# Cross-attention and FFN stack: first-batch clears, weight fetch, key mask, residual adds and squares moved

## What is computed

```python
# L0x (8 heads of 16) and L1x (16 heads of 8): attention of 256 queries on 512 keys
q, k, v = x @ Wq.T + bq, ctx @ Wk.T + bk, ctx @ Wv.T + bv
scores = einsum('bqhd,bkhd->bhqk', q, k) / scale
scores = scores + ((1.0 - attention_mask) * -10000.0)[:, None, None, :]   # L1x only
out = einsum('bhqk,bkhd->bqhd', softmax(scores), v)
# L0f, two layers of local attention and a gated unit
q, k, v = split(shift_token(x) @ wqkv, 3)
q, k = rotary(q / norm(q) * qs, k / norm(k) * ks)     # norm over each head's 64 columns
x = x + local_attention(q, k, v) @ wo                  # window of 64
x = x + (a * gelu(g)) @ w2 + b2                        # a, g from layernorm(shift_token(x))
# L3f: causal attention, 16 heads of 8, and a mixture of experts; both with a residual
```

## Time and profile before

| what | value |
|---|---|
| median of 3 runs | 3030.18 us (3027.31 to 3030.22) |
| the profiled execution | 3025.31 us |
| its span | 3023.5 us |
| mean granted clock of TensorE | 0.893 of full speed |
| PE busy | 2394.9 us, 79% |
| DVE busy | 1631.5 us, 54% |
| ACT busy | 1275.0 us, 42% |
| POOL busy | 941.1 us, 31% |

### The profile page before, as it was taken

How to read it: one execution, slowest core, us unless ns; L and a number is a source line. 1 busy time by engine, 2 the same in 40 slices (tenths; PEclk the granted TensorE clock), 3 DMA queues, 4 the chain that set the end, 5 groups by cost and what they waited for, 6 DMA issues and landing times. The chain is left out here.

```text
span 3023.5 us, 46226 instructions
## 1 busy us (share of the span) xinstructions
PE 2394.9 (79%) x16127; PEld 1479.8 (49%) x16128; DVE 1631.5 (54%) x3753; ACT 1275.0 (42%) x2869; POOL 941.1 (31%) x913
## 2 busy tenths in 40 slices
PE   2973677667655998799749879879999998389698
PEld 1431455345532443566537656546666665245465
DVE  4767764566444775433465444445555554566433
ACT  1652565256522665222214322246666665125222
POOL 1414772377202331000000000037676776044000
PEclk7986898789976999899879889979999999589899
DMA  5610000000012330000010000010000000042000
GB/s 135 81 19 6 1 1 1 0 1 1 1 60 39 45 43 10 15 0 0 0 47 1 1 29 0 0 61 1 1 1 1 1 1 1 5 49 35 1 0 14
DMA packets 49811, 53.80 MB, mean 18 GB/s; under 512 B 9264, under 2 KB 47920, under 8 KB 48720
## 3 DMA queue, kind: packets, MB, share of 16 engines
q1 hardware_dynamic: 42992, 41.68, 8.4%
q0 software_dynamic: 4896, 8.81, 0.9%
q10 hardware_dynamic: 1728, 0.79, 0.2%
HBM read 24.25 MB, written 1.05 MB: 8 GB/s over the span
## 5 line engine op out<-in xcount | busy, mean ns | idle before, releaser
L1946 POOL TENSOR_SCALAR L3x_prob<-L3x_prob,L3x_inverse 128x512 f32<-128x512 f32 x256 | 395.8, 1565 | 184.1 <-DVE L3x_inverse L2124 184.1
L1065 DVE TENSOR_TENSOR W_probT<-W_prob,W_pS 128x512 f32<-128x512 f32 (+1 forms) x232 | 159.4, 687 | 367.9 <-ACT W_prob L1050 367.9
L1050 ACT ACTIVATE W_prob<-W_pS 128x512 f32<-128x512 f32 (+1 forms) x232 | 138.5, 597 | 455.9 <-PE W_pS L1021 455.9
L1031 PEld LDWEIGHTS W_pT<-fw,W_probT 128*128 128x128 f32 (+1 forms) x1856 | 241.9, 191 | 115.9 <-issue 107.4
L1020 PE MATMUL W_pS<-hT,fw 128*128 (+1 forms) x464 | 241.2, 602 | 26.0 <-DVEq L484 26.0
L1031 PE MATMUL W_pT<-fw,W_probT 128*128 128x128 f32 (+1 forms) x1856 | 246.2, 276 | 6.2 <-DVE W_probT L1065 6.2
L2086 DVE CUSTOM_DVE_ANT_0 L3x_prob<-L3x_pS,L3x_mask_now 128x512 f32<-128x512 f32 x256 | 166.0, 686 | 147.5 <-PE L3x_pS L1954 147.5
L1021 PE MATMUL W_pS<-hT,fw 128*128 (+1 forms) x464 | 239.3, 598 | 0.0
L2031 ACT ACTIVATE L3x_prob<-L3x_prob,L3x_row_top 128x512 f32<-128x512 f32 x256 | 183.2, 716 | 73.0 <-DVE L3x_row_top L2086 73.0
L855 DVE TENSOR_REDUCE L1x_row_top<-L1x_pS 128x2 f32<-128x1024 f32 x128 | 156.6, 1223 | 74.3 <-PE L1x_pS L671 73.9
L800 ACT ACTIVATE L1x_prob_by_key<-L1x_pX 128x512 f32<-128x512 f32 x256 | 148.5, 596 | 101.8 <-PE L1x_pX L678 100.5
(11 more groups left out here) (363 smaller groups left out, 5188.6 us busy)
## 6 DMA issues: line engine op xcount, KB each, us to landing
L0x_key_stack<-xw SPq DMA_DIRECT2D x48, 128.0 KB
L1x_key_stack<-xw SPq DMA_DIRECT2D x96, 64.0 KB
L3f_stacks<-L3f_qk_part SPq DMA_DIRECT2D x96, 64.0 KB
fw<-in_f_L3f SPq DMA_DIRECT2D x1, 4483.5 KB, 13.4
fw<-in_f_L1f POOLq DMA_DIRECT2D x1, 4359.0 KB, 13.7
fw<-in_f_L0f POOLq DMA_DIRECT2D x1, 3890.0 KB, 12.4
fw<-in_f_L2f SPq DMA_DIRECT2D x1, 3460.0 KB, 10.8
L0x_query_stack<-xw SPq DMA_DIRECT2D x42, 64.0 KB
```

The source lines that it names most:

```text
L1031: last = pe.matmul(m.pT[:, e % 2, t * C:(t + 1) * C], hidden[0:size, s, t * P:(t + 1) * P], down(i), start=i == 0 and t == 0, stop=i == PI ...
L1050: act.activation(gated[0:size, s, 0:GROUP], prod[0:size, s, :], func, bias=bias).then_inc(activated, 1)
L1065: ins = dve.tensor_tensor(hidden[0:size, s, 0:GROUP], gated[0:size, s, 0:GROUP], prod[0:size, 2 + s, :], ALU.mult)
L1946: pool.tensor_scalar(prob(u, h, t), prob(u, h, t), m.inverse[:, u % 2, h, t:t + 1], None, ALU.mult).then_inc(a.normed, 1)
```

## The change

Five edits. In the narrow attentions DVE clears only the first key buffer ahead of the first query copy, POOL the first query buffer; the other clears follow the copy of batch 0. SP's wait for the clears counts to 2b + 1 in place of 2(b + 1), and ACT's waits for POOL's. The weight fetch goes from POOL's first place to behind the last split step of batch 1. L1x's mask is made and stored in the norm phase, and its phase goes. In the local attentions the squares of the first two batches are made by ACT from PSUM (activation Square, next to the copy), later ones by POOL as before. The two add phases go: the sum is DVE's first operation in the second gated unit of L0f and in L3f's experts, whose output now goes to x. In L3f's attention two of three stack clears, `pO` and the value tile follow batch 0's last add.

```diff
-def prepare(nc, m, name):
+def prepare(nc, m, name, mask=None):
...
+            @ph.block.sync
+            def _(sp):
+                sp.dma_start(m.mask_in[:, :], mask.rearrange("a (p n) -> (a p) n", n=B * SK // P)).then_inc(loaded, 16)
+                sp.wait_ge(steps, 7)
+                for i in range(3):
+                    sp.dma_start(m.key_mask[i:i + 1, :], m.mask_part[:, i, :]).then_inc(stored, 16)
+                sp.wait_ge(stored, 16 * 3)
...
             norm.dve(dve, m, 1, m.x, m.xn, 1e-5)
+            if mask is not None:
+                dve.wait_ge(loaded, 16)
+                split_mask(Steps(dve, steps), dve, m)
             for n, g in ((3, 1), (4, 3)):
...
         if b < 3:
-            sp.wait_ge(a.constant, 2 * (b + 1))
+            sp.wait_ge(a.constant, 2 * b + 1)
...
                     pool.tensor_tensor(to[:, 2, :], rest, to[:, 1, :], ALU.subtract).then_inc(a.split, 1)
+                    if b == 1:
+                        pool.dma_start(*fetch).then_inc(fetched, 16)
...
     act.wait_ge(a.split, 4)
-    act.wait_ge(a.constant, 2)
+    act.wait_ge(a.first_constant, 1)
...
-            pool.dma_start(*fetch).then_inc(fetched, 16)
-            cross_pool(pool, m, a)
+            pool.memset(m.qS[:, 0, :, :], 1.0).then_inc(a.first_constant, 1)
+            cross_pool(pool, m, a, fetch, fetched)
...
-            for n in range(3):
-                dve.memset(m.kS[:, n, :, :], 1.0).then_inc(a.constant, 1)
-                dve.memset(m.qS[:, n, :, :], 1.0).then_inc(a.constant, 1)
-                if n == 0:
-                    dve.memset(m.pO[:, :], 0.0)
-                    dve.memset(m.v[:, :, :, :, :], 1.0).then_inc(a.blanked, 1)
-            dve.wait_ge(a.blanked, 1)
+            dve.memset(m.kS[:, 0, :, :], 1.0).then_inc(a.constant, 1)
...
                     last.then_inc(a.taken_q, 1)
+                    if b == 0:
+                        for i in range(1, 3):
+                            dve.memset(m.kS[:, i, :, :], 1.0).then_inc(a.constant, 1)
+                            dve.memset(m.qS[:, i, :, :], 1.0).then_inc(a.constant, 1)
+                        dve.memset(m.pO[:, :], 0.0)
+                        dve.memset(m.v[:, :, :, :, :], 1.0).then_inc(a.blanked, 1)
+                        dve.wait_ge(a.blanked, 1)
...
+            st = Steps(dve, biased)
+            if residual is not None:
+                st.done(dve.tensor_tensor(wide(x), wide(x), wide(residual), ALU.add))
             if row_bias is not None:
...
-                if at is not None:
+                if at is not None and at[0] >= a.START:
                     b, t = at
                     pool.wait_ge(a.taken_raw, nth(b, t))
-                    if b > 0:
-                        pool.wait_ge(a.summed, nth(b - 1, t))
+                    pool.wait_ge(a.summed, nth(b - 1, t))
                     raw = m.raw[:, t].rearrange("p a n -> p (a n)")
                     pool.tensor_tensor(m.squares[:, t, :], raw, raw, ALU.mult).then_inc(a.squared, 1)
...
+                    if b > a.START:
+                        act.wait_ge(a.squared, nth(b - 1 - a.START, t))
                     if b > 0:
-                        act.wait_ge(a.squared, nth(b - 1, t))
                         act.wait_ge(a.rotated, nth(b - 1, t))
+                    if 0 < b < a.START:
+                        act.wait_ge(a.summed, nth(b - 1, t))
                     for n, bank in enumerate((bankq, bankk)):
                         last = act.activation(m.raw[:, t, n, :], bank, ACT.Copy)
+                        if b < a.START:
+                            last = act.activation(m.squares[:, t, n * W:(n + 1) * W], bank, ACT.Square)
                     last.then_inc(a.taken_raw, 1)
...
-            moe_phase(nc, m, f"L0f{d}_glu", m.xn, [(gate, value, down)], [n for _, n in cut], ACT.Gelu, [None],
-                      biases=(wd["b1"][:, 0:3], wd["b1"][:, 3:6]), row_bias=wd["b2_row"])
-    add_phase(nc, m, "L0f_add")
+            moe_phase(nc, m, f"L0f{d}_glu", m.x if d else m.xn, [(gate, value, down)], [n for _, n in cut], ACT.Gelu, [None],
+                      biases=(wd["b1"][:, 0:3], wd["b1"][:, 3:6]), row_bias=wd["b2_row"],
+                      residual=m.xn if d else None)
...
-            for n in range(3):
-                dve.memset(m.kqS[:, n].rearrange("p j a n -> p (j a n)"), 1.0).then_inc(a.constant, 1)
-                if n == 0:
-                    dve.memset(m.pO[:, :], 0.0)
-                    dve.memset(m.v[:, :, :, :, :], 1.0).then_inc(a.blanked, 1)
-            dve.wait_ge(a.blanked, 1)
+            stack = lambda n: m.kqS[:, n].rearrange("p j a n -> p (j a n)")
+            dve.memset(stack(0), 1.0).then_inc(a.constant, 1)
...
                     dve.tensor_tensor(m.qk[:, :], m.qk[:, :], m.qk_rest[:, :], ALU.add).then_inc(a.taken_turned, 1)
+                    if b == 0:
+                        for i in range(1, 3):
+                            dve.memset(stack(i), 1.0).then_inc(a.constant, 1)
+                        dve.memset(m.pO[:, :], 0.0)
+                        dve.memset(m.v[:, :, :, :, :], 1.0).then_inc(a.blanked, 1)
+                        dve.wait_ge(a.blanked, 1)
...
-    add_phase(nc, m, "L3f_add")
+              list(range(L3F_EXPERTS)), residual=m.xn)
...
-            prepare(nc, m, "L1x")
-            key_mask_phase(nc, m, "L1x", mask_f, False)
+            prepare(nc, m, "L1x", mask_f)
```

More of the change, by code:

```diff
@@ L580, in cross_sync, with cross_pool @@
         sp.wait_ge(a.stacked[n], a.stack_count(last))
-def cross_pool(pool, m, a):
+def cross_pool(pool, m, a, fetch, fetched):
     G = a.GROUP
@@ L930, in _, with split_mask, key_mask_phase @@
             project_pe(pe, m, w["wo"], None, turned, (copied, projected))
-def key_mask_phase(nc, m, name, mask, boolean):
+def split_mask(st, dve, m):
+    part, rest = m.mask_part, m.mask_rest
+    st.done(dve.tensor_scalar(rest[:, 1, :], m.mask_in[:, :], -1.0, 1.0, ALU.mult, ALU.add))
+    st.done(dve.tensor_scalar(rest[:, 0, :], rest[:, 1, :], -10000.0, None, ALU.mult))
+    st.done(dve.tensor_copy(part[:, 0, :], rest[:, 0, :]))
+    st.done(dve.tensor_tensor(rest[:, 1, :], rest[:, 0, :], part[:, 0, :], ALU.subtract))
+    st.done(dve.tensor_copy(part[:, 1, :], rest[:, 1, :]))
+    st.done(dve.tensor_tensor(rest[:, 2, :], rest[:, 1, :], part[:, 1, :], ALU.subtract))
+    st.done(dve.tensor_copy(part[:, 2, :], rest[:, 2, :]))
+def key_mask_phase(nc, m, name, mask):
     n = B * SK // P
@@ L941, in key_mask_phase @@
         loaded, steps, stored = ph.sem("loaded"), ph.sem("steps"), ph.sem("stored")
-        here = m.mask_u8 if boolean else m.mask_in
-        parts = 1 if boolean else 3
+        spread, even_copied, odd_copied = ph.sem("spread"), ph.sem("even_copied"), ph.sem("odd_copied")
+        groups = [m.key_mask[:, n * SK:(n + 1) * SK] for n in range(B)]
         @ph.block.sync
         def _(sp):
[L947 to L969, removed]
+            sp.dma_start(m.mask_u8[:, :], mask.rearrange("a (p n) -> (a p) n", n=n)).then_inc(loaded, 16)
@@ new lines, in _ @@
+            sp.wait_ge(steps, 3)
+            sp.dma_start(m.key_mask[0:1, :], m.mask_part[:, 0, :]).then_inc(stored, 16)
+            sp.wait_ge(stored, 16)
+        @ph.block.tensor
+        def _(pe):
+            pe.wait_ge(stored, 16)
+            for n, group in enumerate(groups):
+                if n >= 4:
+                    pe.wait_ge(odd_copied if n % 2 else even_copied, n // 2 - 1)
+                pe.matmul(m.banks[:, n % 4, :], m.onesb[:, :], group, start=True, stop=True).then_inc(spread, 1)
@@ L971, in _ @@
+        @ph.block.scalar
+        def _(act):
+            for n in range(0, B, 2):
+                act.wait_ge(spread, n + 1)
+                act.activation(groups[n], m.banks[:, n % 4, :], ACT.Copy).then_inc(even_copied, 1)
         @ph.block.vector
@@ L2530, in expert @@
         return gate, value, down
-    moe_phase(nc, m, "L3f_moe", m.xn, [expert(e) for e in range(L3F_EXPERTS)], [n for _, n in cut], ACT.Silu,
-              list(range(L3F_EXPERTS)))
-    add_phase(nc, m, "L3f_add")
+    moe_phase(nc, m, "L3f_moe", m.x, [expert(e) for e in range(L3F_EXPERTS)], [n for _, n in cut], ACT.Silu,
+              list(range(L3F_EXPERTS)), residual=m.xn)
 def store_phase(nc, m, out):
```

45 lines of the change are left out of this document (17 added, 28 removed).

## The result

The changed kernel takes 2988.89 us (median of 4 runs, 2980.16 to 2995.15) against 3030.2 us before: a ratio of 0.9861, 95% interval 0.9836 to 0.9885, or 41 us less. The forecast was 2988, from a sum of 42.4. The total came out as forecast; the parts did not all.

What follows compares the result with a forecast made beforehand. PE, busy for 79% of the span, bounds most stages but stands still at phase starts until the first stacks land. Terms sum to 42.4 us: 3025.3 becomes 2982.9, and by the median, 4.9 higher, the forecast is 2988, range 2971 to 3009.

Steps and rivals of the forecast that it cites:

- L0x: L0x attention: first score 16.28 us earlier, but the fetch delays batch 1's stacks; slot 8 near 75, gain 4.5 us.
- L1x mask: Before L1x: mask steps fit DVE's wait in the norm phase, its own phase goes, PE starts 5.8 us earlier (5 to 7.3).
- L1x attention: L1x attention: query copy 16.3 us nearer its phase's start, less 2 us of fetch delay; gain 14.3 (4.7 to 16.3).
- L3f attention: L3f attention: first copy moves from 2631.42 to 2621.8, behind one clear; gain 9.0 us (8.2 to 9.8).
- local attention: Two local attention phases: two batches' squares on ACT relieve DVE's rotations; 2 us a phase, 4 in all (0 to 7).
- L0f add: Add moved into second gated unit: its phase's 3.0 us saved, about 1.2 comes back by a later first product; 1.8 gained.
- The sum of 44.4: Whole kernel: total gain in us if queues take turns by packet, so stacks wait for only a few fetch packets.
- rival A: No contention between fetch and stacks: L0x gains 13.5 us, L1x all 16.3; sum 53.4, so 2977; chance 0.15.
- the 2 us of delay: L1x attention: the fetch, issued while batch 0's last stacks move, costs 2 us of the 16.3 gained.
- D: Fetch goes in front everywhere: L0x gains 2 us, L1x 4.7, local attention nothing; sum 26.3, so 3004; chance 0.15.
- Rival B: L0x, L1x, L3f: DVE's deferred clears and POOL's split shut each other out; 14.5 us remain, so 3016; chance 0.08.
- Rival C: A stall mid-attention lowers PE's clock; 42 us of slowed work eat the gain, 60 us give 3048; chance 0.04.

## Why the forecast was right, and where not

| term | forecast | measured |
|---|---|---|
| L0x | 4.5 | 2.0; slot 8 3.1 earlier |
| L1x mask | 5.8 | 5.9 (7.40, less 3.03 - 1.56 = 1.47 that the norm phase grew) |
| L1x attention | 14.3 | 16.0 |
| L3f attention | 9.0 | 7.6 and 11.7 |
| local attention | 4 | 3.7, all in the second phase, and not shown to be the edit's |
| L0f add | 1.8 | 2.7 (3.03 - 0.35) |
| L3f add | 3.0 | 2.6; the experts +1.2 and -0.1 |

- **L0x: the mechanism was right.** That the fetch takes its whole length from batch 1's stacks was forecast from L3f's top rows, and the experiments bear it out: 10.8 us come back with the fetch first, and its move alone costs 12.15. The size was off by 1.4 at slot 8, 4.5 against 3.1: not the top row but batch 1's stacks ended last, at 76.9 against 74, since the fetch took 15.4 to land. Of the 3.1, 0.9 were lost by the 17th by-key matmul (59.95 behind the start against 62.13); why was not followed.
- **The rule of the Trainium skill** (DMA: Bandwidth & Descriptors, section Queues, rings and completion order), that a DMA engine takes turns packet by packet, is not contradicted by L0x: turns between packets of such unequal size, 31 KB in the fetch and 0.7 on average in the stacks' queue, would let the fetch through first, and 9 to 21 GB/s beside 334 to 380 are what the stacks got. The mistake was to take the stacks' wait for short because it is a few packets at a time. The sum of 44.4 was not worked through either: it took back only L1x's 2 us and left L0x at 4.5, where the same reading would have given rival A's 13.5.
- **L1x: the term that failed is the 2 us of delay.** It was put at the first score, but the fetch, issued at 905.64, met only the very end of batch 0's stacks; with the fetch last the first score came at 33.21, with it behind batch 1's split at 33.65, 0.4 of delay. Rival A was right in this phase and wrong in L0x; D was wrong in L1x, while its local part, no gain, is not excluded.
- **Mask, adds.** Steps, stores and the 4.17 us of landing and barrier were as forecast. In the second gated unit the product is 1.45 later, as forecast, but only 0.35 of it reaches the phase's end; the text took all of it for lost.
- **Local.** The relief of the rotations (0.69 for 2.38) gave 2.5 to 4 us at the first score of each phase, more than the 2 taken. The first phase lost all of it in its middle, 235.0 against 235.1, and the second was as short in one run without the edit (235.6), with the clock up earlier. The step that the forecast left out is the one from the first score to the phase's end; the 3.7 in the table may be luck.
- **Rival B fell**: the split beside the clears took as long as alone in L0x (1.63 and 1.63) and L3f (1.16 and 1.15), which agrees with the Trainium skill, SBUF — State Buffer, section Who interferes with whom.
- **Rival C did not come with this change**, but with the fetch behind the last split, where one stall and the half clock behind it ate 11 us.
- The close agreement of the totals, 41 and 42.4, is partly luck. L0x came out 2.5 under its term and L1x's attention 1.7 over, the untouched phases took 9.1 us more in one profile and 3.3 in the next. Four runs of the changed kernel spread over 15 us, and their order is nearly that of the granted clock (spans 2993.4, 2990.8, 2983.4 and 2978.4 at 0.893, 0.892, 0.895 and 0.898).

## What to carry to other kernels

A large transfer that nothing needs soon belongs where its queue's engines are idle, not behind the first thing that one wants to protect: here the 10 us ahead of the first stacks were free, and both later places cost some 11 of the 15 to 16 us that the transfer took to land there. Of a change in several parts, try each alone: this one gained 41 us and held a part that loses 10 to 12, and without it the kernel runs at 2967, with ACT's halves exchanged at 2963. And compare PE's granted clock phase by phase, in more than one profile, before a few microseconds are put down to an edit: the local attentions' 3.7 looked like the edit's until a kernel without it showed the same length.

## What was not expected

- A phase of the same code has two or three lengths: L3f's attention 179.4 to 179.6 in three profiles, 176.1 to 176.7 in three and 175.3 in two, with the same code there, and in the two that were compared the clock rose 10 us earlier or later. In L0x a gap of 1 us in place of 3 went with 4 us.
- The stacks of L1x moved at 61 to 112 GB/s at the same share of busy DMA engines (0.59 to 0.62). Which half of the partitions the second queue began with made 78 of 61 with the fetch later; with the fetch first the old order alone gave 66, 74 and 102, the new one 86 and 112. So the halves are not all of it, and why is not settled.
